# Eight weight chunks split between the dense part and the experts, and the last group's routing one tile later

## The reference

```python
hidden = gelu(x @ down_W.T + down_b)                  # 256 -> 64
hidden = hidden @ expert_W[domain_id].T + bias        # 64 -> 64, per item
x1 = layernorm((hidden + domain_emb) @ up_W.T + up_b + x) * gamma + beta
```

```python
h = layernorm(x1) * ln_g + ln_b
h = (h - h.mean(1)) * rsqrt(h.var(1) + 1e-8) * gamma_item + beta_item
gates, idx = top_k(softmax(h @ router_w), 2)          # then normalized to sum 1
hid = relu(h @ exp_w1[e] + exp_b1[e])                 # 256 -> 1024
y += gate * (hid @ exp_w2[e] + exp_b2[e])             # 1024 -> 256
out = x1 + y
```

## Time and profile before

| what | before |
| --- | --- |
| median of 3 runs | 632.25 us (632.22 to 633.03) |
| profiled execution | 628.11 us, its span 626.2 us |
| granted TensorE clock, mean | 0.897 |
| busy: PE, DVE, ACT, POOL | 538.0, 406.6, 276.6, 245.1 us |
| chain that ended last: PE, DVE, POOL, issue, DMA | 56%, 12%, 10%, 8%, 8% |
| stage load, issue to landing, median | 4.5 us (32 of 512 KB) |
| indirect scatter to the queues, issue to landing, median | 2.8 us (64) |
| indirect add to the output, issue to landing, median | 3.8 us (71) |
| `add_bias`, one instruction of two (L1441), mean | 419 ns |

### The profile page before, as it was taken

The page is one execution under the profiler, slowest core; times in us unless marked ns, Lnnn a source line. Parts: engine busy times, 40 slices in busy tenths (PEclk is TensorE's granted clock), DMA queues, the critical chain, the costliest instruction groups (busy, mean ns, idle before and its releaser), DMA issues.

```text
span 626.2 us, 15817 instructions
## 1 busy us (share of the span) xinstructions
PE 538.0 (86%) x4374; PEld 456.2 (73%) x4375; DVE 406.6 (65%) x1454; ACT 276.6 (44%) x628; POOL 245.1 (39%) x208
## 2 busy tenths in 40 slices
PE   5987878887734299999969999999999999999992
PEld 3764656666424188888858888888888888898772
DVE  2566989988898485686654656565656565655671
ACT  3548656756544253333433434343434343433350
POOL 2001388778788505323322322232323333333221
PEclk7679787777866599999998999999999999999997
DMA  9455436564442325334463433333333333323321
GB/s 239 151 171 169 161 106 217 175 218 139 158 157 73 94 85 105 43 38 61 65 162 50 57 44 52 49 51 50 50 54 47 55 46 55 45 40 44 45 35 18
DMA packets 78089, 57.50 MB, mean 92 GB/s; under 512 B 51346, under 2 KB 71699, under 8 KB 77907
## 3 DMA queue, kind: packets, MB, share of 16 engines
q1 hardware_dynamic: 63698, 38.37, 23.0%
q0 software_dynamic: 13296, 17.83, 17.2%
q10 hardware_dynamic: 1058, 0.85, 0.7%
HBM read 23.18 MB, written 24.55 MB: 76 GB/s over the span
## 4 chain that ended last, share of the span: by engine, by line
PE 56%; DVE 12%; POOL 10%; issue 8%; DMA 8%; SPq 3%; ACT 2%; DVEq 0%; POOLq 0%; ACTq 0%
PE banks L794 26%; PE banks L810 24%; DMA out<-xT,token 5%; POOL queues L559 4%; DVE stats L1103 3%; POOL rs L550 3%; DVE w_low L1193 2%; POOL rsT L567 2%; PE banks L633 2%; DMA nb<-queues 1%; DMA uw<-up_b 1%; POOL rs L548 1%; PE banks L693 1%; PE banks L673 1%; SPq L364 1%
## 5 line engine op out<-in xcount | busy, mean ns | idle before, releaser
L794 PE MATMUL banks<-nb,w_high 128*128 128x256 f16 (+1 forms) x1248 | 200.0, 267 | 23.1 <-DMA nb<-queues 22.7
L590 POOL DMA_INDIRECT out<-xT,token x71 | 116.4, 1640 | 257.7 <-DMA out<-xT,token 122.1
L810 PE MATMUL banks<-w_high,stage 128*128 x1136 | 188.3, 273 | 1.2 <-issue 0.3
L794 PE MATMUL banks<-nb,w_low 128*128 128x256 f16 (+1 forms) x624 | 164.9, 266 | 0.0
L810 PE MATMUL banks<-w_low,stage 128*128 x568 | 154.8, 273 | 0.0
L794 PEld LDWEIGHTS banks<-nb,w_high 128*128 x1248 | 115.5, 99 | 43.2 <-issue 24.8
L975 ACT ACTIVATE xb<-banks,feat 128x256 f32<-128x256 f32 (+1 forms) x312 | 118.8, 458 | 43.7 <-PE banks L794 32.9
L810 PEld LDWEIGHTS banks<-w_high,stage 128*128 128x128 f16 x1136 | 110.2, 98 | 15.5 <-issue 2.9
L991 ACT ACTIVATE xT<-act,gate 128x256 f32<-128x256 f32 x71 | 32.6, 501 | 192.9 <-DVE act L1441 167.3
L1410 DVE TENSOR_TENSOR stage<-xb,stage 128x512 f16<-128x512 f32 (+1 forms) x156 | 101.1, 648 | 5.3
L559 POOL DMA_INDIRECT queues<-h_rows,slot x64 | 72.0, 1125 | 40.5 <-DVE slot L1252 23.0
(11 more groups left out here) (183 smaller groups left out, 570.9 us busy)
## 6 DMA issues: line engine op xcount, KB each, us to landing
stage<-expert_w SPq DMA_DIRECT2D x32, 512.0 KB, 4.5
xb<-x SPq DMA_DIRECT2D x8, 512.0 KB, 6.5
out<-rb SPq DMA_DIRECT2D x8, 512.0 KB, 3.2
queues<-pad_row SPq DMA_DIRECT2D x9, 260.0 KB, 2.4
out<-xT,token POOLq DMA_INDIRECT x71, 3.8
queues<-h_rows,slot POOLq DMA_INDIRECT x64, 2.8
rb<-exp_b SPq DMA_DIRECT2D x1, 1024.0 KB, 4.8
nb<-queues SPq DMA_TRANSPOSE x39
```

Source lines behind the costliest of these rows:

```text
L590: nc.gpsimd.indirect_dma_start(out=out, out_offset=bass.IndirectOffsetOnAxis(ap=token[:, i.par, s:s + 1], axis=0), in_=yg[:, i.par, s, :], ...
L794: last = nc.tensor.matmul(ps_in(i, c), w[:, at], features(i)[:, v, k, :], start=(n == 0), stop=(n == 3 * DC - 1))
L810: last = nc.tensor.matmul(ps_out(i.par)[:, s, :], v[:, i.par, c, s * P:(s + 1) * P], w[:, at], start=(n == 0), stop=(n == 3 * FC - 1))
```

## The change

The iterations 1 to 8 of the dense part split two chunks each and no longer three. The eight chunks that are left are loaded by SP after its dense loop, and split behind it: ACT does all eight high parts first, DVE four low parts before the early table and four after it. `loop_end` stands for that place. All four stage slots take part, so the second four loads wait for the first four low parts.

The routing of group 7 moves back. On TensorE `route_and_back` stood between `layer_in(0)` and `layer_in(1)` and now stands behind `layer_out(0)`; `rank` stood ahead of `layer_out(0)` and now ahead of `layer_in(3)`. On ACT `item_norm` moves behind the first layers of tiles 0 and 1, and the adds' gating of tile 0 ahead of the logits. On DVE the item statistics move behind `splits(0)` and `gates(0)`, the scales behind `splits(1)`, and the slots behind `gates(2)`. `late_tiles` moves behind `gates(3)` and so to the other late tables. On POOL the adds of tile 0 go ahead of the scatters of group 7.

```diff
--- before.py
+++ after.py
@@ -54,8 +54,8 @@
 NONE_ROW = ADAPTERS
 CHUNK = 1024
 CHUNKS = 2 * EXPERTS * DC * FF // CHUNK
-CUTS = [8, 3, 3, 3, 3, 3, 3, 3, 3]
-assert sum(CUTS) == CHUNKS and len(CUTS) == GROUPS + 1
+CUTS = [8, 2, 2, 2, 2, 2, 2, 2, 2, 8]
+assert sum(CUTS) == CHUNKS and len(CUTS) == GROUPS + 2
 EARLY = 20
 assert EARLY * SLOTS <= 2 * (TOKENS - GROUP) - EXPERTS * (SLOTS - 1) and EARLY % 2 == 0
 W2_AT = EXPERTS * DC * FF
@@ -421,6 +421,7 @@
         LAST = GROUPS - 1
         last_group = At(LAST // 2, LAST % 2)
         group_before = At((LAST - 1) // 2, (LAST - 1) % 2)
+        loop_end = At((GROUPS + 1) // 2, (GROUPS + 1) % 2)
 
         with nc.Block() as block:
 
@@ -464,6 +465,7 @@
                         sp.dma_start(of(out_rows, s2.g), rb[:, s2.par]).then_inc(x1_stored[s2.par], 16)
 
                 iterations(body)
+                load_weights(loop_end)
 
                 def load(i):
                     row = sp.value_load(tile_row[0:1, bass.ds(i.g, 1)], min_val=0, max_val=IDLE)
@@ -593,11 +595,12 @@
 
                 scatter(group_before, SENDS)
                 item_rstd(last_group)
-                scatter(last_group, SENDS)
                 for par in range(2):
                     pool.wait_ge(x1_stored[par], GROUPS // 2 * 16)
                 pool.wait_ge(spare_stored, 16)
-                for g in range(4):
+                add_rows(tile(0))
+                scatter(last_group, SENDS)
+                for g in range(1, 4):
                     add_rows(tile(g))
                 with pool.Fori(2, WHOLE // 2) as h:
                     add_rows(Tile(h, 0))
@@ -818,14 +821,14 @@
                 pe.wait_ge(hT_ready, GROUPS * DC)
                 pe.wait_ge(centred_ready, GROUPS * GT)
                 layer_in(tile(0))
+                layer_in(tile(1))
+                layer_out(tile(0))
                 route_and_back(last_group)
-                layer_in(tile(1))
+                layer_in(tile(2))
+                layer_out(tile(1))
                 rank(last_group)
-                layer_out(tile(0))
-                layer_in(tile(2))
+                layer_in(tile(3))
                 count(1, GROUPS)
-                layer_out(tile(1))
-                layer_in(tile(3))
                 layer_out(tile(2))
                 with pe.Fori(2, EARLY // 2) as h:
                     for c in (0, 1):
@@ -995,13 +998,14 @@
                     bias_relu(i)
                     choice_ratio(i)
 
-                item_norm(last_group)
+                cut_high(loop_end, slice(None))
                 sc.wait_ge(early_known, 1)
                 first_layer(tile(0))
+                first_layer(tile(1))
+                item_norm(last_group)
+                times_gate(tile(0))
                 logits(last_group)
                 high(last_group)
-                first_layer(tile(1))
-                times_gate(tile(0))
                 first_layer(tile(2))
                 times_gate(tile(1))
                 first_layer(tile(3))
@@ -1448,18 +1452,24 @@
 
                 for k in range(4):
                     place_rows(group_before, k)
+                cut_low(loop_end, slice(0, STAGES))
                 early_table()
+                cut_low(loop_end, slice(STAGES, None))
+                splits(tile(0))
+                gates(tile(0))
                 for c in range(DC):
                     item_parts(last_group, c)
                 for k in range(4):
                     item_variance(last_group, k)
+                splits(tile(1))
                 for c in range(DC):
                     for k in range(3):
                         item_scale(last_group, c, k)
                 item_norm_rest(last_group, False)
                 item_norm_rest(last_group, True)
-                splits(tile(0))
-                gates(tile(0))
+                dve.wait_ge(b2_loaded, 16)
+                add_bias(tile(0))
+                gates(tile(1))
                 best_two(last_group)
                 their_experts(last_group)
                 choices(last_group)
@@ -1467,19 +1477,15 @@
                 both_choices(last_group)
                 low(last_group)
                 row_fields(last_group)
-                splits(tile(1))
-                for k in range(4):
-                    place_rows(last_group, k)
-                dve.wait_ge(b2_loaded, 16)
-                add_bias(tile(0))
-                gates(tile(1))
                 splits(tile(2))
                 add_bias(tile(1))
                 gates(tile(2))
-                late_tiles()
+                for k in range(4):
+                    place_rows(last_group, k)
                 splits(tile(3))
                 add_bias(tile(2))
                 gates(tile(3))
+                late_tiles()
                 late_whole_table()
                 late_half_table()
                 with dve.Fori(2, EARLY // 2) as h:
```

## The result

| what | before | after |
| --- | --- | --- |
| median of 4 runs each, same chip | 632.64 us (632.22 to 633.27) | 643.61 us (642.74 to 646.49) |
| ratio of the two | | 1.0168, 95% interval 1.0128 to 1.0207 |
| profiled execution | 628.11 us | 642.74 us |
| granted TensorE clock, mean | 0.897 | 0.891 |
| slots of the last early scatters known | 199.78 us | 198.35 us |

The change costs 11.0 us by the medians and 14.6 us by the two profiled executions. The forecast was 646.6 us, slower. Lines of the changed kernel lie 2 to 4 further on in the file: L561 are the scatters, L592 the adds, L1197 `cut_low`, L797 `layer_in`, L813 `layer_out`.

What follows compares the result with a forecast made beforehand. Bound by a chain of waits: POOL and DVE, then scatters, then TensorE, broken before tile 10 by adds and SP's fill. -3.3 + 2.1 + 15.6 = +14.4 us gives 642.5 profiled, 646.6 median; 8-in-10 range 636 to 653.

Steps and rivals of the forecast that it cites:

- Dense iterations: Dense part, iterations 1 to 8: one `cut_low` fewer in each gains only the `high`-to-`low` slack, -3.3 us (ends -9.5 and 0).
- The last early scatters: Ahead of tile 0: `cut_low` instructions slow two scatters and delay the early table, so tile 0's load comes 2.1 us later.
- The rule of the Trainium skill that was weighed: DVE beside POOL's scatters: if writing descriptors is not held up by `cut_low`, the forecast is 2.1 us less; judged unlikely.
- The routing: Last group's route on TensorE, after out(0): waits 4.4 us for `item_norm`, then loses 2.5 us to the slower clock.
- The adds: Tiles 1 to 4: tile 1's adds wait behind eight scatters, delaying `gates(3)`, the tables and `splits(4)`, +15.6 us including the route's loss.
- the 4 to 6: TensorE ahead of tile 10: still 4 to 6 us of idle expected in the profile after.
- The second batch of `cut_low`: DVE's last four `cut_low`, after the early table: expected to meet two scatters near 2 us.
- 8 us ahead of out(4): TensorE waiting for `splits(4)` before out(4): about 8 us, its longest idle but one.
- the token copy: DVE's copy in `gates(3)`: expected to wait some 12 us for an add of tile 1.
- The sum: Whole kernel: -3.3 + 2.1 + 15.6 = +14.4 us, so 642.5 us profiled and 646.6 us median.
- the 4.1 us between before's profile and its median: Whole kernel: before's median 632.25 us lies 4.1 above its profiled 628.11; added to 642.5 to forecast 646.6 us.

Runs made afterwards that it cites:

- the warm route: Old order with cuts and spread fill, plus five extra matmuls ahead of each dense route from the second group routed on: 618.59 us against 620.54 without them.
- The adds first: Changed kernel with the last group's eight scatters sent two at a time between the adds of tiles 1 and 2: 633.98 us, ratio 0.9975 to before.
- the statistics early: Changed kernel with the last group's item statistics back ahead of `splits(0)` and the scales ahead of `splits(1)`: 637.89 us, ratio 1.0041 to before.
- the second profile of before: The unchanged kernel before, profiled once more: 636.55 us, tile 0 to tile 10 in 119.4 us against 113.3 in its first profile.
- the cuts alone: Kernel before with only the chunks split as in the change, routing in the old order: 630.14 us against 634.58 for the kernel before.
- the routing alone: Changed kernel with the old three chunks per dense iteration and none behind the loop: 645.81 us, ratio 1.0177 to before.
- the pair with the spread fill: SP's eight queue fills spread behind loads of tiles 6 to 13, in the old order with the cuts (626.20 us) and in the kernel before (630.72 us).
- the kernel with all repairs: Changed kernel with statistics early, late tables spread, adds ahead of or between the scatters, and fill spread: 618.02 us, ratio 0.9747 to before.
- the pair to the warm route: Old order with the cuts and SP's fill spread, without extra matmuls, measured again on the last chip: 620.54 us, ratio 0.9809 to before.
- The three kernels on the last chip: Changed kernel with four order repairs, 618.02 us; old order with cuts and spread fill, 620.54; the latter with five extra matmuls per route, 618.59; before took 632.04.

## Why the prediction was right

**Dense iterations, -3.3 us.** Near in size over many profiles, but taken from a number that is not constant. After's slots came 1.43 us earlier; from the first statistics of iteration 1 to the last early slots the two profiles even take the same, 159.2 and 159.3 us. But one profile is a poor measure: four profiles with three chunks take 159.2 to 162.5, mean 161.1, and eight with two chunks (without the warm route) 153.3 to 160.3, mean 158.6, so -2.5, while single profiles of one kind differ by 3 to 7. I had read the slack between `high` and `low` in one execution and taken it for a constant. It hangs on the clock. In iteration 4, where the earlier trace rows show a slack of 0.04 us, the changed kernel's route ran at half clock, `high` came late, and `low` stood 0.88 us for it, most of the 1.19 us saved:

```profile
116.01 1.23 DVE L1229 TENSOR_TENSOR h_rows<-banks,h_rows 128x1024 f16<-128x1024 f32 x1 [0.88 <-ACT h_rows L907]
```

**The last early scatters, +2.1 us.** From the slots to the load of tile 0 it is 12.6 us with three chunks and 14.4 to 14.7 with two, in every profile read: +2.0. It is made up a little differently: two scatters at +0.98 and +1.01, and no later one caught, where one was forecast. The rule of the Trainium skill that was weighed (page "SBUF — State Buffer", section "Who interferes with whom", which infers that writing descriptors is not held up) does not carry over to `cut_low` here: 1.94 and 1.97 us against 0.96. Whether it is the writing of descriptors or the reading of `slot` that is held, no run shows.

**The routing, 4.4 us of stall and 2.5 us of clock.** Measured 4.05, and a route of 5.7 us from 238.72 to 244.41, as 3.2 + 2.5. From tile 0, in(2) started after 28.26 us; forecast were 28.4.

**The adds, +15.6 us.** Measured from tile 0: the scatters start after 42.7 us (forecast 42.3), `gates(3)` is released after 61.7 (61.4), `splits(4)` starts after 73.0 (72.7), where it was 57.1: +15.9. Tile 10 moved by 15.1 from tile 0 and waited 5.5 us, inside the 4 to 6. "The adds first" takes 8.0 of these 15.1 away and "the statistics early" 6.3, and in the forecast the scatters ahead of the adds made 8.7 and the route 6.9. So this path is the cause.

**What was wrong in it.** Three marks did not come out. The second batch of `cut_low` had no scatter near 2 us. TensorE did not stand 8 us ahead of out(4) but 1.8, and the token copy waited 4.6 us for the add and not 12. The last two are less because TensorE and DVE arrived late by themselves: `add_bias(2)` stood 9.26 us, and TensorE shows 3.3 us of gaps in 266 to 278 us. With the slower clock behind them, in(4) took 11.7 us there (266.42 to 278.14) and not 5.24; without these 6.5 us the wait of 1.8 would have been 8.3. It looks like the stall of the second profile of before. In the changed kernel it lies beside DVE's wait for the adds, which were not held up, and so costs nothing.

**The sum.** +14.4 us forecast, +14.6 between the two profiles, +11.0 between the medians. That the first two agree so well is partly luck: the forecast was built on the one profile of before without the stall, and against the second profile, taken in another round, the changed kernel's is only 6.2 us longer. The parts don't agree as well as the sum either. The new order alone cost 11.2 us by the medians, where its term was 15.6, and the cuts alone gained 4.4, where their two terms come to 1.2. I carried the 4.1 us between before's profile and its median over to the changed kernel. But the median there is only 0.9 us above its profile. The likely reason is that stall: the first profile of before lacks it, the second has it and is 6.1 us longer between tiles 0 and 10, so most runs of before should have paid for it. That is argued from two profiles; no experiment took the stall away on purpose.

**Open.** The cuts alone gained 0.7% (all twelve runs; the pair with the spread fill gives 0.6%) and the routing alone cost 1.8%, which multiplies to 1.011, where 1.0168 was measured. Each of the three is good to about 0.4%, so it is not shown that the cuts gain less in the new order than in the old one. That they gain more than the forecast's 1.2 us in the old one rests on two comparisons, 4.4 and 4.5 us, and has no explanation in the profiles: the dense part gives 2.5 and the scatters take 2.0 back. The runs of the old order with the cuts spread over 16 us, which would fit a stall that they sometimes escape, but that is not shown.

## What to carry to other kernels

When a step is moved back, follow what it holds in each in-order queue, and above all on a queue that works one at a time with a latency: the eight scatters held the adds of tile 1 back by 10 us, and a chain of serial adds stood behind them; put between the adds they cost nearly nothing. A later step can be free if the links of its chain are placed by when each is waited for, as in the kernel with all repairs. Take slack and the offset between profile and median from more than one profile; here one was 4 us off its median and its slacks were not constants.

## What was not expected of the hardware

- A scatter that had started 0.12 us before a run of `cut_low` took its usual 0.96 us (208.20 above), while the two that started inside the first run were stretched, to 1.94 and 1.97 us. But the one at 209.47, within 0.01 us of the start of the second `cut_low`, was not stretched either, and it is the same in the eight other profiles with chunks behind the loop. What decides it is open.
- TensorE is granted 0.50 of its clock in the dense part even when it is busy throughout; this is a window over a route of the pair to the warm route:

```profile
90.30:95.70 5.40, 5.40 (x26) 5.40 (x27) 3.85 (x17) 2.27 (x5) 4.61 (x4) 0.50 0.48 166
```

  Ahead of it TensorE had waited 3.32 us. With the extra matmuls and a wait of 1.82 us the same stretch had a granted clock of 0.74, and one without a wait (168.71 us) 1.00.
- TensorE, ACT and DVE can stand for 3 to 6 us together with no releaser that the profile shows. The three kernels on the last chip have none of it in their profiles, and one of them is a kernel that had it on the chip before (3.8 us of "issue"). Its cause is open.
